# Shared expert of a fused attention and expert block: its float32 matmuls become three fp32r passes, with the splits placed in chosen units

## The reference, cut to what matters

```python
# attention, for each of the 8 heads of 32 features
attn = jnp.tanh(A[:, None] * jnp.einsum('bhnj,bhmj->bhnm', Xc, Xp))
Xh = jnp.einsum('bhnm,bhmk->bhnk', attn, Xp)
...
# last layer: router, then routed experts plus the shared one
logits = xf @ gate_w.T
...
shared = jax.nn.silu(xf @ sw1) * (xf @ sw3) @ sw2
return (shared + routed).reshape(bs, slen, d)
```

## Time and profile before

| | |
|---|---|
| median of 3 runs | 2293.43 us (2288.56 to 2294.23) |
| the profiled execution, its own time | 2285.2 us |
| its span, first to last instruction | 2283.4 us |
| TensorE busy, share of the span | 2039.1 us, 89% |
| VectorE | 1579.8 us, 69% |
| ScalarE | 1216.0 us, 53% |
| mean granted TensorE clock | 0.949 of full speed |
| the attention stage | about 1022 to 1841 us of the span |
| float32 ups of the shared expert, L1340 | 240 instructions into c_p_w, 592 ns each |
| downs, L1359 | 256 instructions, 379 ns median |

### The profile page before, as it was taken

The page is one execution under the profiler, slowest core; times in us unless marked ns, Lnnn a source line. Parts: engine busy times, 40 slices in busy tenths (PEclk is TensorE's granted clock), DMA queues, the critical chain, the costliest instruction groups (busy, mean ns, idle before and its releaser), DMA issues. The chain is left out here.

```text
span 2283.4 us, 40181 instructions
## 1 busy us (share of the span) xinstructions
PE 2039.1 (89%) x12272; PEld 1510.5 (66%) x12272; DVE 1579.8 (69%) x3436; ACT 1216.0 (53%) x1745; POOL 1062.1 (47%) x1214
## 2 busy tenths in 40 slices
PE   7999999938999999977999999999999779999940
PEld 6988888837888888863444444444444468888830
DVE  6777777635666666645788878877887647766747
ACT  4444444405666666644656655556555347767730
POOL 3455555542333332336245554455531347777650
PEclk9999999958999999997999999999999889999975
DMA  7344444134555555524122211222111045655539
GB/s 281 145 169 169 167 167 176 46 146 145 181 183 173 189 172 182 155 90 147 56 93 95 83 57 60 74 77 75 61 37 41 5 141 177 200 167 183 183 135 371
DMA packets 136257, 311.31 MB, mean 136 GB/s; under 512 B 37165, under 2 KB 67986, under 8 KB 132081
## 3 DMA queue, kind: packets, MB, share of 16 engines
q1 hardware_dynamic: 104112, 268.01, 34.9%
q0 software_dynamic: 32064, 42.40, 5.4%
HBM read 203.93 MB, written 152.12 MB: 156 GB/s over the span
## 5 line engine op out<-in xcount | busy, mean ns | idle before, releaser
L1572 ACT ACTIVATE c_att<-c_att 128x1024 f32<-128x1024 f32 x256 | 271.0, 1059 | 245.4 <-DVE c_att L1775 242.8
L1775 DVE TENSOR_TENSOR c_att<-c_p_s,adj 128x1024 f32<-128x1024 f32 x256 | 300.9, 1216 | 68.1 <-PE c_p_o L1321 52.6
L931 POOL DMA_INDIRECT moe_y<-b_y,b_goal x156 | 165.1, 1059 | 343.6 <-DVE b_y L978 305.7
L2028 POOL DMA_INDIRECT moe_y<-d_y,d_goal x256 | 256.7, 1003 | 115.2 <-issue 51.2
L122 PE MATMUL b_p_y<-b_w2h,b_hh 128*128 128x256 f32 x624 | 181.2, 290 | 7.0 <-DVE b_hl L128 6.4
L1308 PEld LDWEIGHTS c_p_s<-c_xcth,c_xpth 32*128 32x128 f32 x512 | 47.6, 183 | 198.1 <-issue 118.1
L128 DVE TENSOR_TENSOR b_hl<-b_ht,b_hh 128x512 fp32r<-128x512 f32 x156 | 108.1, 693 | 100.6 <-ACT b_ht L1071 100.6
L124 PE MATMUL b_p_y<-b_w2h,b_hl 128*128 128x256 f32 x624 | 173.7, 278 | 0.0
L123 PE MATMUL b_p_y<-b_w2l,b_hh 128*128 128x256 f32 x624 | 173.7, 278 | 0.0
L414 POOL DMA_INDIRECT moe_in<-a_xn,a_rows x128 | 142.0, 1109 | 57.5 <-issue 29.2
L1265 POOL DMA_INDIRECT moe_in<-c_xn,c_rows x128 | 132.7, 1037 | 53.7 <-issue 39.3
(11 more groups left out here) (239 smaller groups left out, 6085.4 us busy)
## 6 DMA issues: line engine op xcount, KB each, us to landing
b_w<-in_moe_w SPq DMA_DIRECT2D x78, 512.0 KB, 4.9
moe_in<-b_zeros SPq DMA_DIRECT2D x73, 520.0 KB, 10.8
d_xin<-moe_in SPq DMA_DIRECT2D x64, 520.0 KB, 3.6
adj<-in_adj SPq DMA_DIRECT2D x32, 1024.0 KB, 5.6
b_xin<-moe_in SPq DMA_DIRECT2D x39, 520.0 KB, 6.0
c_g<-moe_y SPq DMA_DIRECT2D x32, 512.0 KB, 4.6
moe_y<-c_zeros SPq DMA_DIRECT2D x32, 512.0 KB, 6.4
d_w<-in_moe_w SPq DMA_DIRECT2D x64, 256.0 KB
```

Of the source, the lines that this page charges most:

```text
L931: pool.indirect_dma_start(out=m["moe0_y"], out_offset=bass.IndirectOffsetOnAxis(ap=goal[:, h, t:t + 1], axis=0), in_=y[:, h, t, :], in_off ...
L1572: act.activation(part, part, ACT.Tanh).then_inc(att_ready, 1)
L1775: dve.tensor_tensor(att[:, u % 2, 2 * c:2 * c + 2, :], p_s[:, 2 * c:2 * c + 2, :], adj[:, h, u % T, :].unsqueeze(1).broadcast_to([P, 2, N] ...
L2028: pool.indirect_dma_start(out=m["moe1_y"], out_offset=bass.IndirectOffsetOnAxis(ap=goal[:, h, t:t + 1], axis=0), in_=y[:, h, t, :], in_off ...
```

## The change

The weights of the shared expert are split once, in unit 1 of graph 0: ScalarE makes three high parts, VectorE three low parts (128x512 each). Each `wide` of the shared expert becomes `up`: two times `exact`, six fp32r matmuls of 128x512. Each `down` becomes twelve fp32r matmuls of 128x256. The normalised input of the shared expert gets a high part beside the float32 one (`evac_turned3`: four copies on ScalarE in unit 3 where there were two) and a low part (`split_turned` on VectorE, 128x1024, in unit 3). The gated activations of each block get a high part (`shared_high`, ScalarE, units 7 and 0) and a low part (`split_shared`, VectorE, 128x512, behind the side work of units 7 and 0). `down(0)` moves from behind the second half of unit 0 to behind the first half of unit 1, after the transposes of L1334 there and ahead of the values. To make room, the attention's output buffer `ot` holds one group in place of two, and the raw weights share the memory of `xn3`.

```diff
@@ attention_phase, TensorE
+            def up(w, c, dst):
+                col = slice(c * P, (c + 1) * P)
+                for k in range(KD):
+                    mm = exact(pe, dst, (w[0][:, k, col], w[1][:, k, col]), (xt3h[:, k, :], xt3l[:, k, :]),
+                               k == 0, k == KD - 1)
+                mm.then_inc(up_done, 1)
...
             def down(c, bank):
                 for t in (2 * c, 2 * c + 1):
+                    tok = slice(t * P, (t + 1) * P)
                     for i in range(KHS):
-                        mm = pe.matmul(by_pair(bank)[:, t % 2, :], sh[:, i, t * P:(t + 1) * P], ws2[:, i, :],
-                                       start=(i == 0), stop=(i == KHS - 1))
+                        mm = exact(pe, by_pair(bank)[:, t % 2, :], (shh[:, i, tok], shl[:, i, tok]),
+                                   (ws2[0][:, i, :], ws2[1][:, i, :]), i == 0, i == KHS - 1)
...
+                    if u == 1 and late:
+                        pe.wait_ge(hs_ready, SH * (b - 1))
+                        pe.wait_ge(xct_lo, GRP * b + GRP)
+                        down(0, z)
...
                 def side_b(u):
-                    if u == 0 and late:
-                        pe.wait_ge(hs_ready, KHS * (b - 1))
-                        pe.wait_ge(xct_lo, GRP * b + GRP)
-                        down(0, z)
                     if u == 1 and late:
                         down(1, w)
...
                     if u == 5 and post:
                         pe.wait_ge(sg_ready, b)
-                        wide(ws1, 0, xt3, w, up_done)
+                        if at_one:
+                            pe.wait_ge(w_split, 8)
+                        pe.wait_ge(xt3_ready, X3 * b)
+                        up(ws1, 0, p_w[:, w, :])
@@ attention_phase, ScalarE
+            def evac_turned3(b, k, bank):
+                act.wait_ge(tr3_done, KD * b + k + 1)
+                act.activation(xt3h[:, k, :], p_w[:, bank, :], ACT.Copy)
+                act.activation(xt3[:, k, :], p_w[:, bank, :], ACT.Copy).then_inc(xt3_ready, 1)
+
+            def shared_high(b, c):
+                act.wait_ge(hs_ready, SH * b + 2 * c + 1)
+                act.activation(shh[:, c, :], sh[:, c, :], ACT.Copy).then_inc(sh_ready, 1)
...
                 def side_b(u):
+                    if u == 0 and post and not is_at(b, 1):
+                        shared_high(b - 2, 1)
                     if u == 0 and post:
                         evac_values(b - 1, 1)
+                    if u == 1 and is_at(b, 0):
+                        split_shared_weights()
@@ attention_phase, VectorE
+            def split_turned(b):
+                dve.wait_ge(xt3_ready, X3 * b + KD)
+                low_part(dve, xt3l[:], xt3[:], xt3h[:]).then_inc(xt3_ready, 1)
+
+            def split_shared(b, c):
+                dve.wait_ge(sh_ready, SH * b + 2 * c + 2)
+                low_part(dve, shl[:, c, :], sh[:, c, :], shh[:, c, :]).then_inc(hs_ready, 1)
...
                         elif not last:
                             apply1(b + 1)
+                        if late:
+                            split_shared(b - 2, 1)
                     if u == 1:
+                        if at_zero:
+                            split_shared_weights()
...
+                    if u == 3 and post:
+                        split_turned(b - 1)
...
                         if not last:
                             split_c(b + 1, 1, w)
+                        if post:
+                            split_shared(b - 1, 0)
```

More of the change, by code:

```diff
@@ L1179, in _ @@
             load_g(0)
-            for dst, name in ((wp[:], "wp"), (bpc[:], "bpc"), (wg[:], "wg"), (ws1[:], "ws1"),
-                              (ws3[:], "ws3"), (ws2[:], "ws2")):
+            for dst, name in ((wp[:], "wp"), (bpc[:], "bpc"), (wg[:], "wg"), (raw[0], "ws1"),
+                              (raw[1], "ws3"), (raw[2], "ws2")):
                 sp.dma_start(dst, a[name]).then_inc(s_w, 16)
@@ L1335, in turn_back, with wide @@
                 mm.then_inc(done, 1)
-            def wide(w, f, src, bank, done, last_of=False):
+            def wide(w, f, src, bank, done):
                 for k in range(KD):
-                    mm = pe.matmul(p_s[:, bank, :] if last_of else p_w[:, bank, :], w[:, k, f * P:(f + 1) * P], src[:, k, :],
+                    mm = pe.matmul(p_w[:, bank, :], w[:, k, f * P:(f + 1) * P], src[:, k, :],
                                    start=(k == 0), stop=(k == KD - 1))
                 mm.then_inc(done, 1)
+            def up(w, c, dst):
[4 more added lines that the diff above has]
+                mm.then_inc(up_done, 1)
             def project_c(par, f, bank):
@@ L1539, in evac_turned, with split_shared_weights @@
                 act.activation(dst[:, k, :], p_w[:, bank, :], ACT.Copy).then_inc(ready, 1)
+            def evac_turned3(b, k, bank):
[5 more added lines that the diff above has]
+                act.activation(shh[:, c, :], sh[:, c, :], ACT.Copy).then_inc(sh_ready, 1)
+            def split_shared_weights():
+                act.wait_ge(s_w, 16 * NL)
+                for dst, src in zip((ws1[0], ws3[0], ws2[0]), raw):
+                    act.activation(dst[:], src, ACT.Copy).then_inc(w_split, 1)
             def evac_projection(b, par, f, bank):
@@ L1556, in evac_values @@
                 act.wait_ge(av_done, UNITS * b + T * f + T)
-                act.activation(ot[:, f, :], p_o[:], ACT.Relu).then_inc(ot_ready, 1)
+                if not (is_at(b, 0) and f == 0):
+                    act.wait_ge(back_done, GRP * b + f)
+                act.activation(ot[:], p_o[:], ACT.Relu).then_inc(ot_ready, 1)
             def exps(b, bank):
@@ L1597, in side_a @@
                         evac_c(b + 1, 1, w)
+                    if u == 7 and post:
+                        shared_high(b - 1, 0)
                 def side_b(u):
+                    if u == 0 and post and not is_at(b, 1):
+                        shared_high(b - 2, 1)
                     if u == 0 and post:
                         evac_values(b - 1, 1)
+                    if u == 1 and is_at(b, 0):
+                        split_shared_weights()
                     if u == 3 and not last:
```

84 lines of the change are left out of this document (50 added, 34 removed).

## The result

The changed kernel takes 2324.5 us (median of 4 runs, 2318.19 to 2330.41), the kernel before 2292.15 us over the four runs beside it. The ratio is 1.0142, with a 95% interval from 1.0112 to 1.0172: slower by 32 us, on the side that was forecast, 13.5 us above the predicted 2311 and inside the range. The profiled execution took 2318.19 us (span 2316.4), 33.0 more than the one of before.

The account below looks back on a forecast made before the run. TensorE was taken to set the pace, with VectorE holding the chain through units 0 and 1. Terms 5.0 + 3 - 1.0 + 3.2 + 0.5 + 8 = 18.7 us gave about 2311 us, range 2290 to 2336.

Parts of the forecast that it names:

- The sum: Whole kernel: terms total 18.7 us, added to the profiled 2285.2 and adjusted to the runs' median, about 2311.
- The ups: Units 5 to 7 on TensorE: each up takes 1.58 instead of 1.92 us, saving 0.34, four per graph.
- The waits: TensorE in each graph: waits 2.0 us for unit 1's scores and 1.1 us more in unit 2.
- Unit 3: Four ScalarE copies, then the new low part: 6.05 us against 5.73 between scores, +0.32 per graph.
- `down(0)` in unit 1: VectorE idles 0.8 us ahead of `add_shared(0)`, waiting for the twelve matmuls: +0.80 per graph.
- The clean loop: Loop graphs without clock falls: each 0.36 us longer (period 47.46), plus 3 us where VectorE's loop turns.
- The clock: Granted clock falls behind TensorE's waits in every second graph, seven for two: +8 us, bounds 0 and +19.
- The end of the stage: Last graph: given no term of its own, counted among fourteen graphs (b = 2 to 15) at +0.36 each.
- the start: First matmul of the stage to the count of b = 2: +2.2 us, with graph 0 +3.2 and graph 1 -1.0.
- the end: Two more copies ahead of the router, two splits ahead of the last downs, against faster ups: +0.5 us.
- Rival 1: Splits hidden and the add's data ready, so all saved matmul time counts: 2267 us, chance 0.13.
- Rival 3: Clock falls in every graph at unit 1's wait, up to 3.2 us each: 2346 us, chance 0.12.

Follow-up runs that it names:

- e5: Kernel before with only the ups in fp32r, xt3's low part moved to unit 4 and the weights' to unit 2 of graph 0: 2274.13 us, ratio 0.9927.
- e3: Kernel before with only the ups in fp32r and the splits of weights and input this takes: 2288.35 us, ratio 0.9997.
- e1: Changed kernel plus eight matmuls with unused results in unit 0, where `down(0)` was: 2307.62 us, ratio 1.0079.
- e7: Whole change with `add_shared(0)` and the low parts of xt3 and weights placed later, plus eight unused matmuls in unit 0: 2275.79 us, ratio 0.9942.
- e2: Changed kernel with `add_shared(0)` moved behind the attention's add and the statistics in VectorE's unit 1: 2310.44 us, ratio 1.0098.
- e4: Changed kernel with its ups back in float32 and without their splits: 2330.67 us, ratio 1.0192.
- e6: Whole change with `add_shared(0)` behind unit 1's statistics, xt3's low part in unit 4, the weights' in unit 2 of graph 0: 2293.85 us, ratio 1.0013.
- e8: Changed kernel with unit 0's low part cut to 8 of 512 columns in graphs 4 to 13: 2313.85 us, ratio 1.0105.
- e10: Kernel before with five unused matmuls added in unit 2 of the last graph only: ratio 1.0005.

## Why the prediction was right, and where it was off

- *The sum.* The step from it to the time slips by 1 us: 2303.9 and 8.2 are 2312.1, not 2311.
- *The ups.* 1.60 us each (1.58 predicted). In e5 the 13 graphs gain 18.3 us; four ups of 1.92 - 1.60 in each make 16.6, and the two falls of before, which it has not, 3.3, together 1.6 more than was gained. Right in the main.
- *The waits.* 2.00 (2.0 predicted), 1.06 (1.1) and 0.31 (0.3) us. The products of unit 1 start at a + 10.07 (10.03 predicted). Right.
- *Unit 3.* 6.10 us from scores to scores (6.05 predicted) in the loop. In the last graph the term was missed: the same split made TensorE wait 2.22 in e3.
- *`down(0)` in unit 1.* The idle time before the add is 2.06, predicted 0.8. The mechanism was right and the size was that of the full clock: the twelve matmuls took 2.70 instead of 1.6, and in b = 8 and 10, where the clock stayed up there, the add waited 0.68 and 0.67. The chain of the graph shown is 10.07 + 9.07 + 1.25 + 28.57 = 48.96, predicted 10.03 + 7.73 + 1.24 + 28.46 = 47.46: all but 0.16 of the difference stands in this one link.
- *The clean loop.* With no fall (e1), 13 graphs are 4.3 us longer than before, which itself holds 3.3 us of falls: 7.6 in all. The prediction had 0.36 x 13 + 3 = 7.7. Right.
- *The clock: the step that was mis-sized.* "I take a fall in every second graph, seven for two: +8 us." It fell in every graph: 22.4 us less the 3.3 of before is +19.1 in the 13 graphs, the upper bound that the prediction gave. The price was near (1.6 predicted; 1.4 for a fall of 3.4 us, 1.7 a graph), the number of graphs wrong by half. The mistake was in how the waits were counted: the 2.0 and 1.1 us were added up against those of before. In e1 and e7 waits of up to 1.3 us made no fall in the 13 graphs, while the waits of 1.9 to 2.2 us in unit 1 had a fall with them in 50 of 52 graphs of after, e2, e4 and e6. The earlier trace rows already held it: 2.06 was followed by a fall, and the new wait was to be 2.0. The Trainium skill, "TensorE: Matmul & The Clock Gate", section "HAM oscillation — how this bites in real kernels", tells of a fall in every tile where the same wait recurs in every tile; this trace agrees, with a fall in 13 graphs of 13, though in two of them it stood behind the second wait and not the first.
- *The end of the stage.* The last graph has TensorE work for fewer units, and was costed as the other thirteen. It took 5.9 us more, with 13.6 us at half clock; this was no term of the sum. Of the twelve kernels the six with 13 us or more at half clock in this graph took 45.2 to 49.7 us for it, the five without a fall there 38.1 to 39.7. The account from 18.7 to 33.0: the clock + 11.1, the last graph + 5.5 (5.9 less its 0.4), the start - 1.2, the end + 0.5, what lies outside - 1.7.
- *The rivals.* Rival 1 (TensorE's saving comes back) was wrong for this order of the work and right for e5. Rival 3 (a fall in every graph) had the right count and twice the measured price: 3.2 us against 1.7. The doubled fall that it was priced by came in four graphs of 13.
- *Luck.* Little: the clock and the last graph erred the same way, 16.6 us together, the start and what lies outside took 2.9 of it back, and the range held what was left.

What stays open: what decides a fall beside the length of the wait. The same 1.30 us in the last graph was followed by a fall in e5 and not in before or e6, the same 1.48 in e8 once and once not, and in the changed kernel 2.20 was not and 1.26 was. These runs do not tell apart what differs. The start up to b = 2 varies from 101 to 112 us with the time at half clock in it, between kernels that run the same program there (after and e1); why that time varies is open too.

## What to carry to other kernels

Before a matmul is moved out of a stretch in which its engine then waits, ask what that wait does to the clock and which instruction stands behind work that will run at half pace; a wait filled with needless work can be cheaper than an empty one (e7 with its eight matmuls is 18 us faster than e6). A saving on the bounding engine came home only where the new splits stand where they wait for nobody, on VectorE behind the statistics rather than behind ScalarE's copies (e5 against e3, 0.7%, in part by two falls fewer). The part of a change that saves nothing on the chain is best left out: the ups alone, placed (0.9927), were no slower than everything, placed and filled (0.9942). And the last iteration is a case of its own, with less work to hide the same wait.

## What had not been expected of the hardware

- More work made the kernel faster: eight matmuls of 128x512 in the 2.0 us wait brought the loop from 644.7 to 622.3 us.
- The length of a wait alone does not say whether the clock falls: in one execution of the changed kernel it stayed up behind 2.20 us and fell behind 1.26.
- A fall in the 13 graphs was over after 3.4 us in nine of them (after); in the last graph it lasted 13.7 us at 0.50 with a wait of 2.22 (e3) and 17.1 behind one of 1.30 (e5).
- The same program up to the count of b = 2 took 111.9 us in one execution and 103.0 in another, with the clock at 0.50 and 0.93 from 1090 to 1116 us (e1, after).
- On one of the chips the kernel before took 2393.47 us against 2287 to 2292 on the others, with the attention stage the same to 1 us (e10: 807.1 us from its first matmul to `d_p_tr`, before 807.6).
